# Counts for the hot nodes of a GNN layer: chunks of 5 nodes by all sources, stored by fifths and streamed back in both layers

## The reference

```python
def _sage_conv(x, src, dst, W_l, b_l, W_r):
    msgs = x[src]
    agg = segment_sum(msgs, dst, num_segments=12500)
    deg = segment_sum(ones(200000), dst, num_segments=12500)
    return (agg / maximum(deg, 1.0)[:, None]) @ W_l + b_l + x @ W_r
h = relu(_sage_conv(x, src, dst, W1_l, b1, W1_r))
h = relu(_sage_conv(h, src, dst, W2_l, b2, W2_r))
out = layernorm(x + (h @ W3 + b3), eps=1e-05)
```

## Time and profile before

| | us |
|---|---|
| median of 3 runs | 3807.28 |
| profiled execution | 3819.06 |
| its span on the core | 3817.3 |
| PE busy | 3027.5 |
| POOL busy | 2390.9 |
| DVE busy | 1670.4 |

### The profile page before, as it was taken

One profiled execution on the slowest core, in us unless ns is written; L12 is line 12 of the kernel. 1 busy time (PEld: TensorE's weight loads), 2 busy tenths in 40 slices (PEclk: granted clock), 3 DMA queues, 4 the chain that ended last, 5 costly groups with the idle time before them and its releaser, 6 DMA issues.

```text
span 3817.3 us, 66644 instructions
## 1 busy us (share of the span) xinstructions
PE 3027.5 (79%) x13648; PEld 2308.9 (60%) x13649; DVE 1670.4 (44%) x4452; ACT 483.5 (13%) x1411; POOL 2390.9 (63%) x2456
## 2 busy tenths in 40 slices
PE   5686787878787888788787678878888788888776
PEld 1362565646565666566576566767677666676665
DVE  7838646464646364544533223333233233323232
ACT  2000010001000000010001011211111111121122
POOL 2452455554655565666667577777777777767675
PEclk7999898999999899999999898999898998999898
DMA  2261454544454555456466565656565565666565
GB/s 74 70 196 54 131 157 139 149 141 147 140 153 124 164 160 158 157 156 190 129 211 213 180 187 180 195 187 200 179 195 177 174 192 183 191 184 190 169 185 171
DMA packets 370797, 623.44 MB, mean 163 GB/s; under 512 B 51411, under 2 KB 281801, under 8 KB 369298
## 3 DMA queue, kind: packets, MB, share of 16 engines
q0 software_dynamic: 117504, 321.02, 28.6%
q1 hardware_dynamic: 172274, 223.09, 17.9%
q10 hardware_dynamic: 80800, 76.82, 6.5%
HBM read 549.71 MB, written 71.02 MB: 163 GB/s over the span
## 4 chain that ended last, share of the span: by engine, by line
PE 30%; POOL 21%; issue 16%; DVEq 11%; DVE 10%; DMA 9%; ACT 2%; ACTq 0%; SPq 0%; PEld 0%; PEldq 0%; POOLq 0%
POOL ring L400 21%; PE psA L474 16%; PE psB L529 5%; DMA ring<-z_rows,scol 3%; DVE oh L889 3%; DVE oh L891 3%; DMA xs<-in_x 3%; PE psY L581 2%; DVEq L871 2%; PE psB L540 2%; DVEq L899 2%; DMA work<-in_x 1%; PE psB L501 1%; DVE oh L859 1%; DMA ring<-in_x,scol 1%
## 5 line engine op out<-in xcount | busy, mean ns | idle before, releaser
L474 PE MATMUL psA<-ring,oh 128*125 128x257 f32 (+1 forms) x6416 | 1685.0, 417 | 437.2 <-DVE oh L859 177.2
L400 POOL DMA_INDIRECT ring<-in_x,scol x1224 | 1186.3, 969 | 935.0 <-PE psA L474 598.4
L474 PEld LDWEIGHTS psA<-ring,oh 128*125 128x125 f32 x6416 | 1289.6, 206 | 782.5 <-issue 564.9
L400 POOL DMA_INDIRECT ring<-z_rows,scol x1224 | 1203.9, 984 | 460.3 <-issue 360.7
L859 DVE SCALAR_TENSOR_TENSOR oh<-dcol,cf,iota 128x500 f32<-128x500 int16 x802 | 596.5, 744 | 1186.5 <-PE psA L474 853.0
L501 PE MATMUL psB<-oh 128*128 128x490 bf16 x1016 | 323.2, 408 | 220.8 <-DVE oh L891 219.0
L891 DVE TENSOR_SCALAR oh<-iota,cf,key 128x490 bf16<-128x490 int16 x1016 | 425.5, 419 | 1.1
L501 PEld LDWEIGHTS psB<-oh 128*128 128x128 bf16 x1016 | 65.4, 100 | 458.4 <-DVE oh L891 444.5
L845 DVE TENSOR_TENSOR acc<-psA,acc x806 | 336.8, 418 | 6.6 <-PE psA L474 6.6
L889 DVE TENSOR_SCALAR oh<-iota,key 128x128 bf16<-128x128 int16 x1016 | 270.9, 267 | 131.6 <-issue 109.6
L529 PE MATMUL psB<-xs,cnt_a 128*125 128x257 f32 x980 | 245.5, 395 | 28.9 <-DMA xs<-in_x 28.8
(11 more groups left out here) (125 smaller groups left out, 1322.4 us busy)
## 6 DMA issues: line engine op xcount, KB each, us to landing
xs<-in_x SPq DMA_DIRECT2D x120, 512.0 KB, 4.4
cnt_a<-z_rows SPq DMA_DIRECT2D x70, 768.0 KB
counts<-cnt_a SPq DMA_DIRECT2D x10, 3185.0 KB, 12.6
cnt_a<-counts SPq DMA_DIRECT2D x70, 455.0 KB
work<-in_x ACTq DMA_DIRECT2D x200, 125.0 KB
ring<-in_x,scol POOLq DMA_INDIRECT x1224, 6.6
ring<-z_rows,scol POOLq DMA_INDIRECT x1224, 6.8
h_cols<-hT ACTq DMA_DIRECT2D x100, 125.0 KB, 4.1
```

The lines of the kernel that those rows point to most:

```text
L400: pool.indirect_dma_start(ring[:, slot, b, 0:D], None, rows_dram, bass.IndirectOffsetOnAxis(scol[:, n - C0:n - C0 + 1], 0)).then_inc(rows_ ...
L474: mm = pe.matmul(psA[0:WN, bass.ds(bank, W)], oh[:, 2 * (slot % 2) + later, b, :], ring[:, slot, b, 0:W], start=(b == 0), stop=(b == nb - 1))
```

## The change

Chunks are 5 nodes by all 98 source blocks, held as 100 (`JP`): 25 chunks a window, 500 columns, rounds of 2 blocks, with 4 slots of 2 blocks whose place comes from a register. Five chunks make a fifth (`PARTS` = 5, `PW` = 25 nodes), which is stored to DRAM as 1.28 MB. The copy from `psB` turns the order, so that in SBUF 5 source blocks lie next to each other for each node.

Layer 0 is now: 5 times 8 groups with the build of window 0 alone; for windows 0 to 3, twice 4 plain groups and then 5 times 8 groups that build a fifth of the next window and do 4 dense steps of this one; for window 4 the same without a build; 5 times 4 groups, each followed by four fallback steps; 6 groups. In an eight, chunks are marked after groups 0, 2, 3, 4 and 5 and copied after groups 2 to 6, dense steps come after groups 0, 2, 3 and 5. Layer 1 has 10 times 4 plain groups and then the schedule of window 4 for all five windows. A dense step has 5 source blocks, 20 steps a window; its counts are read back from DRAM in both layers, as 5 runs of 500 bytes on each of 128 partitions. The weights of a dense matmul are then every fifth value. The dense product has a PSUM bank of its own, `psD`, taken from the ring of products, which has 3. `finish` is called after each four or eight.

```diff
-CD = 10
+CD = 5
+CH = WN // CD
+JP = 100
+CJ = CD * JP
+PART = 5
+PARTS = CH // PART
+SJ = 5
+STEPS = JP // SJ
+SLOTS = 4
+DENSE, MARK, KEEP = (0, 2, 3, 5), (0, 2, 3, 4, 5), (2, 3, 4, 5, 6)
+BANKS = 3
...
-        psA = psum("psA", [P, 4 * 512])
+        ps4 = psum("ps4", [P, 4 * 512])
+        psA, psD = ps4[:, 0:BANKS * 512], ps4[:, BANKS * 512:]
...
+        counts = scratch[:, 0:u].rearrange("p (t n j) -> p t n j", n=PW, j=SJ)
+        lin_a = scratch[:, u:u + 2 * SJ * WN].rearrange("p (q f n j) -> p q f n j", q=2, f=PARTS, j=SJ)
...
+            def load_step(rows_dram, w, t):
+                q = t % 2
+                place(q)
+                sp.dma_start(lin_a[:, q].rearrange("p f n j -> p f (n j)"),
+                             a_dram[w * PARTS:(w + 1) * PARTS, :, t * SJ * PW:(t + 1) * SJ * PW].rearrange(
+                                 "f p n -> p f n")).then_inc(s_lin[q], 16)
+                load_rows(rows_dram, t, s_lin[q])
+
+            def store_part(w, f):
+                sp.wait_ge(s_bank, credit[s_bank] + w * CH + (f + 1) * PART)
+                sp.dma_start(a_dram[w * PARTS + f], scratch[:, 0:JP * PW]).then_inc(s_kept, 16)
...
+            for w in range(HW):
+                sp.wait_ge(s_kept, credit[s_kept] + 16 * PARTS * (w + 1))
+                for t in range(STEPS):
+                    load_step(x, w, t)
+                    if t % 4 == 1 and t > 1 and w + 1 < HW:
+                        store_part(w + 1, t // 4 - 1)
+                if w + 1 < HW:
+                    store_part(w + 1, PARTS - 1)
...
+                for k in range(SJ):
+                    mm = pe.matmul(psD[0:WN, 0:W], lin_a[:, q, :, :, k].rearrange("p f n -> p (f n)"), lin_x[:, q, k, 0:W],
+                                   start=(t == 0 and k == 0), stop=(t == 3 and k == SJ - 1))
...
+                def eight(builds, dense):
+                    for i in range(8):
+                        one_group(i)
+                        if dense and i in DENSE:
+                            dense_step(l, DENSE.index(i))
+                        if builds and i in MARK:
+                            chunk(CJ)
+                    finish(until)
...
+                with pe.Fori(0, STEPS // 4):
+                    four()
+                    with pe.Fori(0, 2):
+                        fallback(l, 0)
+                        fallback(l, 1)
...
+                v.tensor_copy(counts[:, :, k * CD:(k + 1) * CD, :],
+                              psB[:, 0:CJ].rearrange("p (t j d) -> p t d j", j=SJ, d=CD)).then_inc(s_bank, 1)
...
+                def eight(builds, w):
+                    for i in range(8):
+                        group(l, i, GB)
+                        if builds and i in KEEP:
+                            keep_counts(KEEP.index(i))
+                        if builds and i in MARK:
+                            hot_chunk()
+                    finish(until)
+                    if w is not None:
+                        v.reg_add(xdone, xdone, 4)
+                        v.wait_ge(s_xused, v.snap(xdone, min_val=1, max_val=1 << 24))
+                        add_hot(l, v.snap(w, min_val=0, max_val=HW - 1))
```

More of the change, by code:

```diff
@@ L377, in _ @@
-            all_blocks(z_dram, n1 + HW * FC)
+            for w in range(HW):
+                for t in range(STEPS):
+                    load_step(z_dram, w, t)
+            fallback(z_dram)
         @block.gpsimd
@@ L402, in _ @@
                             bass.IndirectOffsetOnAxis(scol[:, n - C0:n - C0 + 1], 0)).then_inc(
-                                rows_end[l] if g == NGG - 1 and b == GB - 1 else rows[l][slot], 16)
+                                rows[l][slot], 16)
         @block.tensor
@@ L494, in group @@
                 pe.reg_add(gi, gi, -4 if i % 2 else 4)
             def count_blocks(n, first):
-                for slot in range(2):
-                    pe.wait_ge(s_hot, pe.snap(hot, min_val=1, max_val=1 << 24))
-                    for b in range(2):
-                        mm = pe.matmul(psB[:, 0:n], oh1[:, slot, b, 0:P], oh1[:, slot, b, P:P + n],
-                                       start=first and slot == 0 and b == 0, stop=True, skip_group_check=True)
-                    mm.then_inc(s_cnt, 1)
-                    pe.reg_add(hot, hot, 1)
@@ new lines, in count_blocks @@
+                pe.wait_ge(s_hot, hv)
+                pe.reg_add(hot, hot, 1)
+                for b in range(2):
+                    mm = pe.matmul(psB[:, 0:n], oh1[:, bass.ds(at[2 * b], P)], oh1[:, bass.ds(at[2 * b + 1], n)],
+                                   start=first and b == 0, stop=True, skip_group_check=True)
+                mm.then_inc(s_cnt, 1)
+                pe.reg_add(slot_n, slot_n, 1)
+                pe.reg_alu(slot_n, slot_n, SLOTS - 1, ALU.bitwise_and)
+                pe.reg_alu(slot_at, slot_n, SW, ALU.mult)
@@ L551, in fallback @@
                 with pe.If(HW < end):
                     with pe.Fori(HW, end):
[L553 to L560 removed]
+                        for h in range(2):
+                            chunk(FN)
+                            if h == 0:
+                                pe.reg_add(at_row, at_row, -2)
@@ L680, in layer, with four @@
-                with pe.Fori(0, FC // 2 - 1):
+                def four():
                     for i in range(4):
                         one_group(i)
-                        if i % 2:
-                            fallback(l)
-                            finish(until)
-                for i in range(NGG - REST % 4, NGG):
-                    one_group(i)
-                    if i >= NGG - 2:
-                        fallback(l)
+                    finish(until)
[7 more added lines that the diff above has]
+                    finish(until)
@@ L690, in layer @@
+                with pe.Fori(0, STEPS // 4):
+                    four()
+                    with pe.Fori(0, 2):
+                        fallback(l, 0)
+                        fallback(l, 1)
+                for i in range(TAIL_GROUPS):
+                    one_group(i % R)
                 pe.reg_mov(until, NW)
@@ new lines, in layer @@
+                if l == 0:
+                    with v.Fori(0, PARTS):
+                        eight(True, None)
+                    with v.Fori(0, HW - 1) as w:
+                        with v.Fori(0, 2):
+                            four()
+                        with v.Fori(0, PARTS):
+                            eight(True, w)
+                else:
+                    with v.Fori(0, 2 * PARTS):
+                        four()
+                with v.Fori(HW - 1 if l == 0 else 0, HW) as w:
+                    with v.Fori(0, 2):
+                        four()
+                    with v.Fori(0, PARTS):
+                        eight(False, w)
@@ L1054, in layer @@
+                fallback_start()
+                with v.Fori(0, STEPS // 4):
+                    four()
+                    with v.Fori(0, 2):
                         fallback(l)
+                        fallback(l)
+                for i in range(TAIL_GROUPS):
+                    group(l, i % R, GB)
                 add_product(l)
```

508 lines of the change are left out of this document (215 added, 293 removed).

## The result

| | before | after |
|---|---|---|
| median of four runs, us | 3805.84 | 3909.86 (3901.61 to 3911.61) |
| profiled execution, us | 3819.06 | 3911.61 |
| its span on the core, us | 3817.3 | 3909.8 |
| first gather of layer 1, us | 2150.96 | 2069.38 |

The ratio of the times is 1.027, 95% interval 1.0234 to 1.0305. 3470 us was forecast, 3370 to 3660 as the range, and 0.05 as the chance of slower. The change lost 2.7% where 8.9% was to be gained. The new kernel's layer 0 is 82 us shorter, not 344. Its layer 1, which was to stay at 1673 us, takes 1840 instead of 1666.

The account below looks back on a forecast made before the run. Layer 1 was taken as bound by POOL's issuing of gathers, layer 0's parts by DVE, then PE. Layer 0's stages summed to 1807 us, plus 1673 for layer 1: span 3480, so 3470 us forecast, range 3370 to 3660.

Parts of the forecast that it names:

- bursts of up to 4 windows (3.1 + 3 x 4.3 = 16 us), which the ring with its 3 groups, 15 us, just covers: Layer 0's finishing of windows every 8 groups: POOL's ring of gathered groups just covers PE's 16 us; 268 us per 48 groups.
- the burst and the fallbacks in fours add about 5: Layer 1: finishing windows in a row and grouped fallback steps add about 5 us, within 1673 us for the layer.
- 0 to 5.8 us for each of 25 returns; I take 4: DVE in layer 0's building eights: each loop return stalls 0 to 5.8 us, taken as 4, 100 us in the sum.
- some 6 us for PE in each 20 us: End of layer 0, 20 groups with four fallbacks behind each four: PE waits some 6 us for rows; 107 us for the stretch.
- I take 0.55 us for DVE: Marking counts on DVE in layer 0: 0.55 us for each of 540 blocks, bounds 0.5 and 0.9.
- stage B: Layer 0, four times 48 groups, mostly with one window's dense steps and the next's build: 268 us each, 1072 in all.
- One PSUM bank less in the ring of products costs nothing: Product ring between PE and DVE: one bank fewer costs nothing, as DVE adds product c - 2 before making operand c + 1.
- (1): DVE becomes the bound, the 500-column compare losing speed or the strided copy doubling: 3550 to 3660 us, middle 3600, chance 0.24.
- (2): POOL alone bounds layer 0, with three engines overlapping fully and returns costing nothing: 3360 us, chance 0.10.
- (3): Strided weight loads slow PE's dense steps in both layers: 3750 us at 0.42 us a load, 3900 at 0.5, chance 0.06.
- weight loads above 0.22 us: Sign in PE's dense steps, weight loads longer than 0.22 us, that would show the forecast wrong through slow strided weights.
- (4): Nothing gained: 500-byte count loads land late behind SP's waits, stalling PE at each window start and eight: 3720 to 3800, chance 0.05.

Follow-up runs that it names:

- e1: Changed kernel with finish called after every second group in the fours and eights, on PE and DVE: 3677.61 us, ratio 0.9651 to the kernel before.
- e4: Kernel before with finish made rarer, after every fourth group in layer 0's parts and every eighth in layer 1: 4071.97 us, ratio 1.0693.
- e3: Changed kernel with the 25 building eights of layer 0 written out on DVE instead of looped: 3834.68 us, ratio 1.0066 to the kernel before.
- e10: Changed kernel with finish after every second group, fallback steps spread and DVE's 25 building eights written out: 3557.14 us, ratio 0.9332 to the kernel before.
- e9: Changed kernel with finish after every second group and one fallback step after each of the last 20 looped groups: 3652.32 us, ratio 0.9586 to the kernel before.
- e12: Kernel before with a ring of 3 product banks instead of 4: 3837.89 us, ratio 1.0078.
- e2: Changed kernel with dense weights taken as 125 neighbouring values instead of every fifth, summing wrong values: 3909.09 us, ratio 1.0266 to the kernel before.
- e11: Changed kernel with finish after every second group and counts read in runs of 2500 bytes instead of 500: 3671.5 us, ratio 0.9632 to the kernel before.

## Why the prediction was wrong

The span was to be 3480 and was 3909.8, 430 us more: 262 in layer 0 (2069 for 1807) and 168 in layer 1 (1840 for 1673). By the steps of the prediction:

1. **"bursts of up to 4 windows (3.1 + 3 x 4.3 = 16 us), which the ring with its 3 groups, 15 us, just covers"**, and "the burst and the fallbacks in fours add about 5" for layer 1. This is the step that failed, and it is worth 232 us (e1), 177 of them in layer 1, the part that was thought safe. Three things in it were wrong. The ring's three groups are room for POOL from the moment that it has issued the group PE takes next, and the gathers' landing and PE's last pair use up part of it: of 15 us, 8.0 were left in the eight above, though PE came to the burst with nothing left to take from the ring. This is why even bursts of two windows, 12.1 us at most, stopped POOL. The burst was also priced with PE's instructions alone, 4.3 us a window from layer 0's end, while PE's stop ends with DVE's next operand, behind the same windows and ScalarE's roots (15.0 us for 11.7; 15.0 less 8.0, and the 1.5 us to POOL's restart, is the stop of 8.49). And layer 1 had 1564.6 us of gathers in 1665, so any stop of POOL goes to the end: its 5 us was not worked out from anything. e4 shows the same in the kernel before.

2. **The returns of the loops, "0 to 5.8 us for each of 25 returns; I take 4".** The mechanism was right, the size was not: 5.8 us on average over the 23 jumps in the trace, and written out they give 75 us (e3, 87 of them in layer 0 less 11 in layer 1) to 95 us (e10). The sum had them inside a DVE total of 246 us beside 250 of PE, as if they lay under the others' work; like the bursts they stop PE, as the ring of operands is two groups deep. The rule of the Trainium skill, Runtime: NRT & Kernel Launch, section "Instruction fetch mechanics", was the better guide: by it all the returns pay, and in the trace the 6.19 us above is one of 23 of its kind, while e3, with no jump back there, has none.

3. **The clusters of fallbacks, "some 6 us for PE in each 20 us".** In the timeline of PE in the kernel after three of layer 0's clusters end in waits of 12.1 to 14.1 us for rows. Spreading them gave 25 us (e9 against e1). In layer 1, where they were inside "the burst and the fallbacks in fours add about 5", POOL stood 46 us at the five.

```profile
1906.01 11.66 PE L486 MATMUL ps<-ring,oh 128*125 128x257 f32 x40 [12.13 <-DMA scratch<-in_x]
1938.07 11.01 PE L486 MATMUL ps<-ring,oh 128*125 128x257 f32 x40 [12.44 <-DMA scratch<-in_x]
1966.21 12.54 PE L486 MATMUL ps<-ring,oh 128*125 128x257 f32 x48 [14.06 <-DMA scratch<-in_x]
```

4. **"I take 0.55 us for DVE" a block.** The compares kept their speed, but over 415 pairs of neighbouring blocks the mean from one start to the next is 0.72 us (0.52 in the kernel before, over the 876 pairs less than 1.5 us apart). Two blocks of one round from the timeline of DVE:

```profile
108.81 0.25 DVE L904 TENSOR_SCALAR oh<-iota,key 128x128 int16 x1 [0.32 <-issue]
108.98 0.41 DVE L906 TENSOR_SCALAR oh<-iota,cf,key 128x500 int16 x1
109.31 0.25 DVE L904 TENSOR_SCALAR oh<-iota,key 128x128 int16 x1
109.47 0.41 DVE L906 TENSOR_SCALAR oh<-iota,cf,key 128x500 int16 x1
110.19 0.25 DVE L904 TENSOR_SCALAR oh<-iota,key 128x128 int16 x1 [0.31 <-issue]
```

A round of two takes 1.38 us, with a gap between rounds in which nothing is shown. Its group has 109.5 us of such gaps. 540 x (0.72 - 0.55) = 92 us of DVE's time were missing in the sum. That is close to what e10 still lies above the forecast in layer 0 (1900 for 1807: 37 up to the end of the first 48 groups after stage A, 13, 21 and 6 in the three spans of stage B after it, 8 each in stage C and at the end), but this was read, not tried: that the gaps make up this difference is not shown, and no kernel with larger rounds was run. Its layer 1 takes 1656 us, 17 less than named.

5. **"One PSUM bank less in the ring of products costs nothing."** In the kernel before it cost some 22 us (e12). What it costs in the new order wasn't tried, since no bank is free there.

What held: the counts of blocks, pairs and windows; compare and copy at the low ends of their bounds; the dense step of 10 records in 2.17 us, 0.217 a record (2718.57 to 2720.74 below); no slower gathers; stores and loads of counts without a stall at the start of a window (outside the fallback clusters PE waited for none of SyncE's loads in layer 0).

```profile
2718.57 2.33 PE L546 MATMUL ps<-scratch 128*125 128x256 f32 x10
2720.74 3.62 PE L486 MATMUL ps<-ring,oh 128*125 128x256 f32 x16
```

The rivals: (1) fell with its premises, the compare at 432 ns and the copy at 677 ns. (2), 3360 us, is nowhere near. (3) was the only slower one, and its 3750 to 3900 us lie near the measured time by luck, as it fell too: the load is 295 ns and thus above the 0.244 us at which a step was to lose time, and yet the records keep 0.217 us. The sign "weight loads above 0.22 us" was badly chosen, as the duration of a load that overlaps says nothing of the pace; only the distance between matmuls does. The rule of the Trainium skill, SBUF — State Buffer, section "Door 1: The DMA port swizzle", agrees with the longer load (the kernel before's dense loads took 196 ns in layer 0 and 187 in layer 1; here 295 against e2's 196), and for this kernel it decides nothing. (4) fell: the runs of 500 bytes cost nothing that e11 could show, and outside the fallback clusters no load of SyncE's held PE up in layer 0. The mechanism that made the kernel slower stood in the text with a price of 5 us and no rival to it. A rival "the bursts stop POOL in layer 1, which has no slack" could have been stated from the same rows: three windows are 11.7 us by the prediction's own prices, the pair or two ahead of them 1.7 to 3.5 us, and that uses up the 15 us of the ring before a gather's landing is counted.

In spans, the change with its loops closed as in e10 takes some 260 us off the 3817 us of before. The way in which they were closed instead cost 350 us (after against e10). How much of the 260 is the counting itself isn't shown, since e10 also takes away returns of a kind that the kernel before has the earlier trace rows.

## What to carry to other kernels

When a consumer stops, its filler can go on only for the room that is free when the stop begins, and that is less than the depth of the ring, even if the consumer has caught up: here 8.0 of 15 us. Where the filler is the bound, the part of the stop beyond this room is not made up. Price the length of the stop by the engine that ends it, not by the one that is stopped. When loops are made longer so that they branch less often, look at what sat at the old loop's end (here `finish`): its calls come in bunches, and they hit the stage without slack, even if it is not the stage being changed. A duration of an overlapped instruction is no evidence of cost; take the distance between those that it is hidden under.

## What the runs showed of the hardware

- At each of 23 jumps back over 8 groups and 5 chunks DVE stood 4.6 to 7.3 us, 5.8 on average, with nothing to wait for. Written out (e3), the same work has no such gap, and jumps back over 8 groups without chunks in layer 1 show 1.5 to 2.6 us.
- An f32 weight load with a step of 20 bytes took 295 ns and a contiguous one in the same place 196, both at the same pace of matmuls, 0.217 us a record.
- A PSUM read by DVE with a step of 5 f32 values, 500 a partition, took 677 ns, a contiguous one of 490 took 669.
- 102,400 packets fewer on SyncE's queue for the same 254.08 MB (e11 against e1) took its share from 22.4% to 21.6%, and the time stayed within its interval.
